# Perceiver block on one core: projection halves and value batches in an even order, a third bank for row maxima, slot-only gate products made early, slot batches in pairs

## What is computed

```python
x = x + xattn(ln(x), ctx)      # 16 heads of 16, 256 queries, 4096 keys, softmax, Wo, bo
x = x + attn(ln(x))            # 16 heads of 16, causal, keys and queries normalised per head
x = x + ffn(ln(x))             # below, T = 256 tokens, 64 slots, top 8
# ffn
h = gelu([x, slot_mean] @ w1 + b1)
logits = (h @ w2 + b2) / (|tau| + 0.1)
alpha = softmax over the 8 largest of 64, 0 elsewhere          # 256 x 64 per batch
si = alpha^T x / sum(alpha)                                    # 64 x 256
gi, gh = si @ Wih^T + bih, slots @ Whh^T + bhh                 # 768 columns
r, z = sigmoid(gi_r + gh_r), sigmoid(gi_z + gh_z)
n = tanh(gi_n + r * gh_n);  S = (1 - z) n + z slots
y = ln(S + softmax(q k^T / 8) v) * g + b                       # q, k, v from S
out = alpha (y @ wvp + bvp) @ wo + bo
```

## Time and profile before

| | us |
|---|---|
| median of 3 runs | 1363.12 (1356.85 to 1363.43) |
| the profiled execution's own time | 1364.89 |
| its span, first to last instruction | 1362.8 |
| PE busy | 1264.0 (93%) |
| DVE busy | 852.3 (63%) |
| ACT busy | 734.1 (54%) |
| POOL busy | 157.0 (12%) |
| mean granted clock of TensorE | 0.954 |

### The profile page before, as it was taken

The page is one execution under the profiler, slowest core; times in us unless marked ns, Lnnn a source line. Parts: engine busy times, 40 slices in busy tenths (PEclk is TensorE's granted clock), DMA queues, the critical chain, the costliest instruction groups (busy, mean ns, idle before and its releaser), DMA issues.

```text
span 1362.8 us, 26201 instructions
## 1 busy us (share of the span) xinstructions
PE 1264.0 (93%) x10286; PEld 735.7 (54%) x10286; DVE 852.3 (63%) x1563; ACT 734.1 (54%) x1324; POOL 157.0 (12%) x191
## 2 busy tenths in 40 slices
PE   5899999999999999999999999979999887896987
PEld 4685565555555555555555555434444464455534
DVE  4567776777777777776777777767773058534222
ACT  2133666766666666766666766656678712241111
POOL 5432121111111111111111110100000140000000
PEclk9898999999999999999999999999999989997666
DMA  8562434443433434333433433262220000000000
GB/s 235 156 168 66 109 94 111 114 108 102 109 100 100 118 99 109 98 103 102 116 105 102 110 82 89 57 176 64 60 60 1 2 1 0 2 3 1 0 0 31
DMA packets 153046, 111.18 MB, mean 82 GB/s; under 512 B 18409, under 2 KB 152123, under 8 KB 152893
## 3 DMA queue, kind: packets, MB, share of 16 engines
q1 hardware_dynamic: 151293, 107.93, 29.7%
q10 hardware_dynamic: 1600, 1.31, 0.3%
HBM read 81.25 MB, written 27.79 MB: 80 GB/s over the span
## 4 chain that ended last, share of the span: by engine, by line
PE 81%; DVE 11%; ACT 4%; issue 2%; DMA 1%; SPq 1%; POOL 0%; ACTq 0%; DVEq 0%
PE acc L1338 18%; PE mx L1285 17%; PE st L1297 14%; PE kps L1248 6%; PE kps L1257 6%; DVE mxp L896 6%; PE st L1257 2%; ACT prob L794 2%; DVE kst L1061 2%; PE acc L1248 1%; PE setB L1539 1%; PE st L1214 1%; PE setB L1533 1%; PE st L1467 1%; DMA kst<-kscr 1%
## 5 line engine op out<-in xcount | busy, mean ns | idle before, releaser
L896 DVE TENSOR_REDUCE mxp<-mx 128x1 f32<-128x512 f32 x1024 | 666.6, 686 | 287.5 <-PE mx L1285 286.3
L1285 PE MATMUL mx<-kst,qst 96*128 96x512 bf16 x1024 | 394.2, 385 | 31.2 <-DMA qst<-qscr 8.4
L1297 PE MATMUL st<-qst,kst 99*128 99x256 bf16 x2048 | 389.8, 274 | 3.6 <-ACT prob L728 1.8
L728 ACT ACTIVATE prob<-st 128x512 f32<-128x512 f32 x512 | 284.5, 600 | 148.9 <-PE st L1297 147.3
L1297 PEld LDWEIGHTS st<-qst,kst 99*128 99x128 bf16 x2048 | 177.3, 98 | 212.1 <-ACT prob L728 46.1
L728 ACT ACTIVATE xnT<-st 128x512 f32<-128x512 f32 x256 | 147.0, 596 | 82.6 <-PE st L1297 79.0
L728 ACT ACTIVATE xn<-st 128x512 f32<-128x512 f32 x256 | 145.7, 602 | 79.8 <-PE st L1297 79.4
L1285 PEld LDWEIGHTS mx<-kst,qst 96*128 96x128 bf16 x1024 | 99.0, 97 | 94.8 <-DVE mxp L896 66.0
L1338 PE MATMUL acc<-prob,v_raw 128*17 128x256 f32 x2048 | 135.4, 382 | 1.8 <-ACT prob L728 1.3
L513 POOL CAST kraw<-kraw 128x512 bf16<-128x512 f32 x54 | 32.9, 609 | 653.8 <-DVE kraw L846 653.8
L1257 PE MATMUL kps<-wv,ctx 128*128 128x256 f32 (+1 forms) x376 | 96.7, 378 | 0.0
(11 more groups left out here) (374 smaller groups left out, 1034.2 us busy)
## 6 DMA issues: line engine op xcount, KB each, us to landing
kst<-kscr SPq DMA_DIRECT2D x128, 192.0 KB, 3.0
kst<-kscr SPq DMA_DIRECT2D x384, 64.0 KB, 2.8
kscr<-kraw SPq DMA_DIRECT2D x108, 192.0 KB, 2.6
ctx<-in_ctxT SPq DMA_DIRECT2D x93, 128.0 KB, 2.5
ctx<-in_ctxT SPq DMA_DIRECT2D x93, 64.0 KB, 2.3
kscr<-o_sb SPq DMA_DIRECT2D x20, 192.0 KB, 2.5
v_raw<-in_ctxT SPq DMA_DIRECT2D x3, 512.0 KB, 7.1
qscr<-v_raw SPq DMA_DIRECT2D x12, 128.0 KB, 2.1
```

What stands on the lines that cost most here:

```text
L728: act.activation(exps(n), st[n % 3][:, :], ACT.Exp).then_inc(exp_done, 1)
L896: dve.reduce_max(at, mxb[n % 2][:, :], AX.X).then_inc(max_red, 1)
L1285: pe.matmul(mxb[n % 2][:, :], qst[0:96, 4 * (q % 3) + j, qt * P:(qt + 1) * P], kst[0:96, j, at:at + 512], start=True, stop=True).then_inc( ...
L1297: mm = pe.matmul(st[n % 3][:, h * T:(h + 1) * T], kst[0:99, j, at:at + P], qst[0:99, 4 * (q % 3) + j, :], start=True, stop=True)
```

## The change

1. The projection halves stand at t % 8 = 0 and 4, ACT's copies at unit 5 and DVE's subtraction at unit 6 of the same group.
2. From unit `NP` = 828 of the maxima on (made beside score unit 752, behind the last projection) the banks are `mx0`, `mx1` and `kps`, and from 830 a product waits for the reduction of n - 3.
3. The slot mean, tau and the scaled b2 are made by DVE before the heads are turned; the product of the slot mean and the slot-only products of the gates are made once, between the first block's addition and the second `turn`; ACT copies them to `gpre`. In the feed-forward part an identity product brings them into the banks, and r * gh_n reads `gpre`.
4. b2 is added by DVE with the scaling of the logits; bo is added to `x_sb` by POOL like the other two.
5. Slot sums alternate between the two batches of a pair; alpha's transposes of a pair share the partitions; values, scores and output products work on a pair of batches (128 slots), with a mask `apart` of -1e30 between the two; the scores come before the values; the last products read half the partitions each.
6. Two activations of one column, Gelu and Exp, stand ahead of the waits for their data.

```diff
+NP = 11 * UQ + 48 + AHEAD
+        def bank_of_max(n):
+            return mxb[n % 2] if n < NP else (mxb[0], mxb[1], kps)[(n - NP) % 3]
@@ sync: setup and the small inputs
-            for n, name in enumerate(("L0_xattn_bo", "L0_attn_bo")):
+            for n, name in enumerate(("L0_xattn_bo", "L0_attn_bo", "L0_ffn_bo")):
...
+                        sp.dma_start(b2t[:, :], a["L0_ffn_b2"].rearrange("(o n) -> o n", o=1)
+                                     .to_broadcast([P, SL])).then_inc(small_in, 16)
@@ gpsimd
+            add_bias(2)
@@ scalar: the loop
-                if n >= 8 and t % 8 == 0:
-                    c = k_job((n - 8) // UQ, (n - 8) % UQ // 8)
+                if t % 8 == 5:
+                    c = k_job(q, t // 8)
                     if c is not None:
                         k_first(c)
-                    c = v_job((n - 8) // UQ, (n - 8) % UQ // 8)
+                    c = v_job(q, t // 8)
@@ scalar: the tail
             norm_sd(1)
+            for n in range(2):
+                act.wait_ge(g_pre_ps, 1)
+                act.activation(gpre[:, n * 512:(n + 1) * 512], (mxb[1], acc)[n][:, :], ACT.Copy).then_inc(g_pre_out, 1)
             turned(2)
...
             turned(3)
+            act.activation(pre[:, :], epsc[:, :], ACT.Gelu)
...
+            act.activation(pre[:, :], epsc[:, :], ACT.Exp)
@@ vector: the loop
-                dve.reduce_max(at, mxb[n % 2][:, :], AX.X).then_inc(max_red, 1)
+                dve.reduce_max(at, bank_of_max(n)[:, :], AX.X).then_inc(max_red, 1)
...
-                if n >= 8 and t % 8 == 2:
-                    c = k_job((n - 10) // UQ, (n - 10) % UQ // 8)
+                if t % 8 == 6:
+                    c = k_job(q, t // 8)
@@ tensor: the loop
-                wait(pe, max_red, n - 1)
+                wait(pe, max_red, n - 1 if n < NP + 2 else n - 2)
+                if n == NP + 2:
+                    pe.wait_ge(v_out, NCH)
+                    pe.wait_ge(k_r, NCH)
...
-                if t % 8 in (4, 7):
-                    g = (t % 8 - 4) // 3
+                if t % 8 in (0, 4):
+                    g = t % 8 // 4
@@ tensor: before the second turn
             pe.wait_ge(x_new, 4)
+            pe.wait_ge(sm_out, 2)
+            for c in range(2):
+                pe.matmul(misc[:, 8:9], wt["L0_ffn_w1"][:, 2 + c, :], smean[:, 1, c:c + 1], start=(c == 0), stop=False)
+            pe.matmul(misc[:, 8:9], bias["L0_ffn_b1"], ones[0:1, 0:1], start=False, stop=True)
...
+            for c in range(2):
+                pe.matmul(mxb[1][:, :], slotT[:, c, :], whh[:, c, 0:2 * D], start=(c == 0), stop=False)
+            for n, row in enumerate((bih, bhh)):
+                pe.matmul(mxb[1][:, :], ones[0:1, 0:P], row[:, 0:2 * D], start=False, stop=(n == 1))
+            pe.matmul(acc[:, 0:D], ones[0:1, 0:P], bih[:, 2 * D:3 * D], start=True, stop=True)
+            for c in range(2):
+                pe.matmul(acc[:, D:2 * D], slotT[:, c, :], whh[:, c, 2 * D:3 * D], start=(c == 0), stop=False)
+            pe.matmul(acc[:, D:2 * D], ones[0:1, 0:P], bhh[:, 2 * D:3 * D], start=False, stop=True).then_inc(g_pre_ps, 1)
             turn(2, normed, ln_xn, lambda t: NT + t + 1)
@@ tensor: the gates
-                for c in range(2):
-                    pe.matmul(rzb[:, :], slotT[:, c, :], whh[:, c, 0:2 * D], start=(c == 0), stop=False)
-                for row in (bih, bhh):
-                    pe.matmul(rzb[:, :], ones[0:1, 0:P], row[:, 0:2 * D], start=False, stop=False)
...
+                pe.matmul(rzb[:, :], ident[:, :], gpre[:, 0:2 * D], start=True, stop=False)
+                pe.matmul(nb[:, 0:D], ident[:, :], gpre[:, 2 * D:3 * D], start=True, stop=False)
...
-            for b in range(B):
-                rows = slice((b % 2) * SL, (b % 2 + 1) * SL)
+            for p in range(2):
                 for q in range(2):
-                    pe.matmul(st[b // 2][rows, 0:D], alpha[:, 2 * b + q, :], xn[:, 2 * b + q, :],
-                              start=(q == 0), stop=(q == 1))
+                    for e in range(2):
+                        pe.matmul(st[p][e * SL:(e + 1) * SL, 0:D], alpha[:, 4 * p + 2 * e + q, :],
+                                  xn[:, 4 * p + 2 * e + q, :], start=(q == 0), stop=(q == 1), skip_group_check=True)
@@ tensor: the end
+            for r in range(2):
+                pe.wait_ge(svo_out, r + 1)
                 for j in range(2):
+                    for e in range(2):
+                        half = slice(e * SL, (e + 1) * SL)
+                        mm = pe.matmul(last[2 * r + e][:, j * D:(j + 1) * D], alphaT[half, r, j * P:(j + 1) * P],
+                                       svo[half, r, :], start=True, stop=True)
+                        if j:
+                            mm.then_inc(out_ps, 1)
```

More of the change, by code:

```diff
@@ L1594, in _ @@
                 mm.then_inc(out_ps, 1)
-            pe.wait_ge(sm_out, 2)
             pe.wait_ge(x_new, 8)
-            for c in range(2):
-                pe.matmul(kps[:, 0:1], wt["L0_ffn_w1"][:, 2 + c, :], smean[:, 1, c:c + 1], start=(c == 0), stop=False)
-            pe.matmul(kps[:, 0:1], bias["L0_ffn_b1"], ones[0:1, 0:1], start=False, stop=True).then_inc(cv_ps, 1)
             turn(3, normed, ln_xn, lambda t: 2 * NT + t + 1)
@@ L1678, in _ @@
             mm.then_inc(qk_ps, 1)
-            pe.wait_ge(alT_out, 2)
-            for b in range(B):
-                to = (mxb[1], acc)[b // 2][0:SL, (b % 2) * D:(b % 2 + 1) * D]
-                for c in range(2):
-                    pe.matmul(to, snT[:, c, b * SL:(b + 1) * SL], wt["L0_ffn_wv"][:, c, :], start=(c == 0), stop=False)
-                mm = pe.matmul(to, ones[0:1, 0:SL], bias["L0_ffn_bv"], start=False, stop=True)
-                if b % 2:
-                    mm.then_inc(v4_ps, 1)
@@ new lines, in _ @@
+            pe.wait_ge(qk_out, 2)
+            for r in range(2):
+                mm = pe.matmul(mxb[0][:, r * P:(r + 1) * P], qkT[:, 0, r * P:(r + 1) * P], qkT[:, 1, r * P:(r + 1) * P],
+                               start=False, stop=True, skip_group_check=True)
+            mm.then_inc(c_ps, 1)
+            for r in range(2):
+                for c in range(2):
+                    mm = pe.matmul(mxb[1][:, r * D:(r + 1) * D], snT[:, c, r * P:(r + 1) * P], wt["L0_ffn_wv"][:, c, :],
+                                   start=(c == 0), stop=(c == 1))
@@ L1692, in _ @@
+            mm.then_inc(v4_ps, 1)
+            for r in range(2):
+                pe.matmul(kps[:, r * D:(r + 1) * D], ones[0:1, 0:P], bias["L0_ffn_bv"], start=(r == 0), stop=False,
+                          skip_group_check=True)
             pe.wait_ge(c_out, 1)
             for r in range(2):
-                tr = pe.transpose(misc[0:SL, r * P:(r + 1) * P], att[:, r, :], ident[:, :])
+                tr = pe.matmul(misc[:, r * P:(r + 1) * P], att[:, r, :], ident[:, :], start=True, stop=True)
@@ L1701, in _ @@
             mm.then_inc(cm_ps, 1)
             last = (st[2], mxb[0], misc, kps)
-            for n in range(4):
-                if n == 3:
-                    pe.wait_ge(y_out, 1)
-                pe.matmul(last[n][:, 0:D], ones[0:1, 0:P], bias["L0_ffn_bo"], start=True, stop=False)
             pe.wait_ge(ln_xn, 3 * NT + 2)
```

152 lines of the change are left out of this document (72 added, 80 removed).

## The result

| | before | after |
|---|---|---|
| median of 4 runs, us | 1359.98 (1355.36 to 1363.43) | 1289.84 (1286.84 to 1294.19) |
| span of the profiled execution, us | 1362.8 | 1288.6 |
| mean granted clock | 0.954 | 0.965 |

The ratio is 0.949 (95% interval 0.944 to 0.953): 70.1 us less, where 70 were forecast. Forecast were 1293.0 us, in 1280 to 1309; that the time lies 3 us under it is the kernel before, whose median is 1359.98 with a fourth run and was 1363.12 without it.

The account below looks back on a forecast made before the run. The prediction took TensorE's work to bound the projection loop, with one bubble per group, and two banks to bind the later units. Loop 34 plus tail 36 made 70 us off 1364.9: 1294.9, median 1293, range 1280 to 1309.

Parts of the forecast that it names:

- Bound by PE with one bubble per group: Key loop with projections: groups take 7.73 us for 7.44 of work; even order removes the 0.29 us wait, saving 19 us.
- Third bank: Late key loop without projections: three banks take four units from 3.30 to 2.85 us; 18 us saved, longer stall returns 1.7.
- The first rival: Key loop: the 0.29 us wait moves to another unit instead of going, costing the 19 us: 1312 us; chance 0.12.
- The third: Rival, key loop: projections' first halves wait for DVE or ScalarE; at 1.1 us DVE lag, 1366 us, slower; chance 0.02.
- Tail: Everything behind the key loop: nine terms for feed-forward part, slot attention and last products sum to 36 us saved.
- early slot-only products: PE's idle gap before the second transposes: products end 2.3 us late, but faster transposes at full clock make up for it: nothing.
- third normalising to the slot sums: Feed-forward part: 4.3 us earlier transposes, 1.3 table load, 3.5 one-row products, 12.2 slot sums directly behind alpha.
- slot sums: Feed-forward part: alternating between two column halves overlaps the products, 7.0 us becomes 3.5; 3 us saved.
- slot attention: Tail: scores come before values, at 1319.0 instead of 1329.3, and the attention's transposes start earlier; 7.6 us saved.
- output weights and last products: End of the tail: eight output-weight products become four, 2.4 us; last sixteen become eight in two row halves, 3.5 us.
- the Gelu table's 1.3: Feed-forward part: a 1.28 us table load between the first product and Gelu moves ahead, saving 1.3 us.
- The second rival: Tail falls to half clock and the column halves do not overlap, costing 14 us: 1307 us; chance 0.15.

Follow-up runs that it names:

- e1: The kernel before with the even order of projection halves alone (behind units with t % 8 = 0 and 4): 1341.71 us, ratio 0.984.
- e2: The kernel before with the third bank of maxima alone, from the last projected chunk on: 1345.02 us, ratio 0.986.
- e5: The changed kernel with the thirteen late weight loads issued one per group of eight score units instead of all at once: 1284.06 us, ratio 0.944.
- e4: The changed kernel with DVE's key subtraction one unit later (t % 8 = 7 in place of 6): 1341.73 us, ratio 0.984 to the kernel before.
- e6: The changed kernel with its early slot-only gate products split, the 512-column part moved to the gap behind the second additions: 1289.65 us, ratio 0.950.
- e8: The changed kernel without the Gelu table's early load and without alternating slot sums, each bank's 256-column products kept together: 1287.79 us, ratio 0.948.
- e11: The changed kernel with the slot sums' products in the order of the kernel before, one-column products between the column halves: 1288.91 us, run once.
- e9: The changed kernel with Exp ahead of ScalarE's copy of the values, and value and key bias rows in TensorE's gaps around the new slots' transposes: 1285.90 us.
- e7: The changed kernel with Exp ahead of ScalarE's values copy and query, key and value bias products ahead of the wait for turned slots: 1293.65 us.
- e3: The changed kernel with the loop put back (old projection positions, two banks of maxima), keeping the part behind the loop: 1327.67 us, ratio 0.974.

## Why the prediction was right

The mechanisms were right, and the sum (70 forecast, 70.1 between the medians) is closer than its parts: the loop gave 36.5 us of 34 forecast, the tail 34.0 of 36. That the two cancel is luck.

- **Bound by PE with one bubble per group**: right. 7.44 forecast, 7.43 measured; 1.8 us a round forecast, 1.86 measured. Rounds 0 to 10 went from 690.6 to 670.6 us: 20.0 against 19 - 0.9. e1 shows that the order does it alone (rounds 0 to 10 in 669.3). The first group took 9.88 us (8.64 before), but 8.1 to 9.9 in the other traces, so the 0.9 at half clock is not shown as a loss of the order.
- **Third bank**: right. Four units 2.85 forecast; a plain group of eight takes 5.69. Rounds 11 to 14 gained 16.6 against 18 - 1.7. The stall grew from 6.18 to 7.24 in these two traces; e2 and the others confirm that it eats part of the gain, e5 that it came from the bunch of weight loads and nothing deeper.
- **The first rival** (bubble moved): not seen, no wait of PE for DVE from 200 to 500 us. **The third** (the projection waits): e4 shows its price, 48 us, and that it starts less than one unit away. The 0.3 us by which I had the cover longer than the need is what the trace has too (0.25 to 0.32). I had priced the lag of 1.1 us at 73 us over 91 groups; only the halves behind key chunks can wait, so half as many.
- **Tail**, 36 forecast and 34.0 measured, by pieces (distances between starts in the two traces):

| piece | forecast | measured |
|---|---|---|
| up to the second attention's products (slot-only products early) | 0 | -2.6 |
| from there to the third normalising | 0 | -1.4 |
| third normalising to the slot sums | 21.3 | 22.1 |
| slot sums | 3 | 2.3 |
| gate products | -1.9 | -1.3 |
| slot attention | 7.6 | 6.9 |
| output weights and last products | 5.9 | 7.9 |

The largest gain, the slot sums directly behind alpha (12.2 forecast; the gap went from 12.20 to 0.05 us), stands in these rows of the changed kernel, with the third transposes, which began 0.55 us behind the normalised rows' start:

```profile
1211.97 5.05 PE L1233 MATMUL st<-ident,xn 128*128 128x128 f32 x24 [5.05 <-DVE xn L880]
...
1230.88 0.69 DVE L1156 TENSOR_TENSOR v_raw<-v_raw,lsum 128x512 f32<-128x512 f32 x1
...
1231.62 1.98 PE L1664 MATMUL st<-xn,v_raw 128*64 128x256 f32 x8 [4.63 <-DVE v_raw L1156]
```

The term that failed is "nothing" for the early slot-only products. I had them end 2.3 us late, they ended 3.3 us late, and I had set the transposes' faster clock against it. The transposes took 5.5 us in place of 6.2 and not 3.9: the clock fell to half at 1066.3, as they began, though PE had idled nowhere since 1058.7 (narrow products until 1060.2, four of 128 rows until 1062.1, mostly one-row products from there). e6 puts the term right: from unit 1023 to the second attention's products it takes 27.0 us, the kernel before 27.9, the changed kernel 30.5. Within the 21.3 the Gelu table's 1.3 was too much (e8: 0.5), and the Exp preload's worth was not tried. Of the slot sums' 3 us 2.3 came, but not from alternating (e8, e11). In slot attention I took the values as what the transposes wait for; the row shows Exp behind the copy as well, and e9 gets about 2.7 us more from the same products by their order.
- **The second rival** (half clock without overlap): halves overlap, as the end's timeline shows in pairs of products 0.01 us apart:

```profile
1281.21 0.48 PE L1757 MATMUL st<-kst 64*128 64x256 f32 x1
1281.22 0.48 PE L1757 MATMUL mx<-kst 64*128 64x256 f32 x1
```

The clock averages 0.70 from the third normalising on, against 0.65 in the earlier trace rows, and not under 0.55. Cutting PE's work there did not lower it; why it rose was not tried.

## What to carry to other kernels

An engine that looks 98% busy can still have a bubble: compare starts with the sum of the work, instruction by instruction, and put the long products between the short ones that need another engine's answer. Before filling an idle gap of one engine, measure the gap to the end and at the clock that rules there; filler that is wider than the gap by 3.3 us is on the path for all of it, and half of it in the next gap costs nothing (e6; e9 against e7 for bias rows). Instructions in one queue should stand in the order in which their data come, transfers too: thirteen loads in one bunch cost 9.5 us in the changed kernel, spread out none. Where a step frees a bank for another engine, measure how long before the need it ends (0.3 us here): waits do not show it until it is gone (e4).

## What the runs showed that I had not expected

- The same code can fall on either side of a change of the clock: four products of 512 columns (L1486) took 1.98 us in the changed kernel and 3.51 in e9, where the clock fell 18.1 us behind unit 1023 in place of 24.3. The second transposes started 2.4 us later for it (26.6 against 24.2). Of the eight kernels here with the unsplit products five have the first pattern and three (e3, e5, e9) the second.

```profile
1061.10 3.51 PE L1486 MATMUL mx<-v_raw,wq 128*128 128x512 f32 x4
```

- The start, up to score unit 0, takes 124.7 to 129.4 us in the traces of kernels that do not differ there, as much as several of the gains tried here.
- One unit in DVE's position decides over 48 us (e4), with nothing in the changed kernel's waits that shows how near the edge is; the starts of DVE and PE show it, 0.3 us.
